# Reordering VectorE's work in an attention stage, and staging its queries in four tiles

## What is computed

```
qh, kh, vh = proj(layernorm(x), Wq, bq), proj(ctx, Wk, bk), proj(ctx, Wv, bv)   # (b, h, s, dk=16, m=4), 16 heads
qh, kh, vh = t + 0.1 * amp * einsum('bhsdi,hij->bhsdj', t, interference)         # for each t of the three
scores = einsum('bhqdm,bhkdm->bhqkm', qh, kh) / sqrt(dk)
out = einsum('bhqkm,bhkdm->bhqdm', softmax(scores, axis=3), vh)
x = x + tanh(g_xattn) * (out @ Wo.T + bo)
y = layernorm(x)
x = x + tanh(g_ffn) * (y @ W_org.T + sum_e coeffs[b, e] * (y @ down[e]) @ up[e])
```

## Time and profile before

| what | before |
|---|---|
| median of 3 runs | 1434.46 us (1432.31 to 1436.73) |
| profiled execution: its own time | 1435.46 us |
| profiled execution: span from first to last instruction | 1433.4 us |
| TensorE busy, share of the span | 1375.1 us, 96% |
| VectorE, ScalarE, GpSimd busy | 672.0, 399.9, 385.8 us |
| mean granted TensorE clock | 0.983 |

### The profile page before, as it was taken

One profiled execution on the slowest core, in us unless ns is written; L12 is line 12 of the kernel. 1 busy time (PEld: TensorE's weight loads), 2 busy tenths in 40 slices (PEclk: granted clock), 3 DMA queues, 4 the chain that ended last, 5 costly groups with the idle time before them and its releaser, 6 DMA issues.

```text
span 1433.4 us, 22180 instructions
## 1 busy us (share of the span) xinstructions
PE 1375.1 (96%) x8464; PEld 1139.6 (80%) x8464; DVE 672.0 (47%) x1370; ACT 399.9 (28%) x728; POOL 385.8 (27%) x584
## 2 busy tenths in 40 slices
PE   7999999999999999779999999999989999999998
PEld 6888888888788888658877888888767878878787
DVE  5333131231855554456666666767766343143110
ACT  3310111111322222234555455555442120121100
POOL 1079990000500000124555565555500000000000
PEclk9999999999999999769999999999999999999999
DMA  5784655636567878976777777775542212202001
GB/s 196 206 223 159 137 150 141 159 133 142 145 190 178 189 165 220 267 209 185 234 211 212 226 208 227 214 214 175 192 153 82 89 45 88 74 31 82 35 31 58
DMA packets 181864, 224.99 MB, mean 157 GB/s; under 512 B 24064, under 2 KB 122496, under 8 KB 181760
## 3 DMA queue, kind: packets, MB, share of 16 engines
q1 hardware_dynamic: 165376, 187.62, 46.1%
q10 hardware_dynamic: 16384, 35.97, 8.0%
HBM read 137.02 MB, written 85.46 MB: 155 GB/s over the span
## 4 chain that ended last, share of the span: by engine, by line
PE 83%; DMA 6%; DVE 5%; issue 2%; SPq 1%; ACT 1%; POOL 0%; ACTq 0%; POOLq 0%; DVEq 0%
PE bank L160 19%; PE bank L162 19%; PE bank L161 19%; PE bank L991 5%; PE bank L976 4%; PE bank L956 4%; DMA early_q<-neg 3%; PE bank L937 3%; PE bank L939 3%; PE bank L938 3%; PE bank L300 2%; PE bank L334 2%; DMA q_in<-neg 2%; DMA q_rows<-stage_hi 1%; DVE raw_o L1139 1%
## 5 line engine op out<-in xcount | busy, mean ns | idle before, releaser
L1057 ACT ACTIVATE probT<-bank 128x512 f32<-128x512 f32 x256 | 139.0, 596 | 100.9 <-PE bank L976 97.2
L1099 DVE TRANSPOSE_TENSOR_REDUCE part<-bank 128x16 f32<-128x512 f32 x256 | 164.3, 672 | 1.9 <-PE bank L956 1.9
L520 DVE SCALAR_TENSOR_TENSOR stage_lo<-bank,bias_mixed,stage_hi 128x512 fp32r<-128x512 f32 x64 | 47.9, 749 | 229.4 <-ACT stage_hi L522 229.4
L160 PE MATMUL bank<-place_a,w_hi 128*128 128x512 f32 x384 | 151.0, 393 | 1.8 <-DVE place_a L153 1.8
L162 PE MATMUL bank<-place_a,w_lo 128*128 128x512 f32 x384 | 149.6, 390 | 0.0
L161 PE MATMUL bank<-place_a,w_hi 128*128 128x512 f32 x384 | 149.5, 389 | 0.0
L522 ACT ACTIVATE stage_hi<-bank,bias_mixed 128x512 fp32r<-128x512 f32 x64 | 44.1, 690 | 273.7 <-PE bank L162 256.1
L937 PE MATMUL bank<-place_a,oT_hi 128*128 128x512 f32 x256 | 108.6, 424 | 0.5 <-POOL oT_lo L1187 0.4
L1443 DVE SCALAR_TENSOR_TENSOR raw_d<-bank,gates,raw_d 128x512 f32<-128x512 f32 x32 | 24.0, 750 | 173.4 <-PE bank L162 173.4
L160 PE MATMUL bank<-place_a,yT_hi 128*128 128x512 f32 x256 | 102.4, 400 | 0.0
L1112 DVE TENSOR_REDUCE negmax<-bank 32x32 f32<-32x128 f32 x128 | 35.6, 278 | 140.0 <-PE bank L963 140.0
(11 more groups left out here) (209 smaller groups left out, 2826.1 us busy)
## 6 DMA issues: line engine op xcount, KB each, us to landing
k_rows<-stage_hi SPq DMA_DIRECT2D x128, 128.0 KB, 2.5
v_pad<-v_out SPq DMA_DIRECT2D x32, 512.0 KB, 2.6
v_place<-v_pad ACTq DMA_DIRECT2D x32, 512.0 KB, 4.9
q_rows<-stage_hi SPq DMA_DIRECT2D x124, 128.0 KB, 2.5
q_in<-q_rows SPq DMA_DIRECT2D x128, 100.0 KB
k_in<-k_rows SPq DMA_DIRECT2D x64, 196.0 KB
early_q<-q_rows SPq DMA_DIRECT2D x90, 100.0 KB
k_rows<-stage_lo SPq DMA_DIRECT2D x64, 128.0 KB, 2.5
```

Source lines behind the costliest of these rows:

```text
L160: nc.tensor.matmul(bank_ap, sh, mh, start=(i == 0), stop=False)
L520: lambda bank: nc.vector.scalar_tensor_tensor(out=lo[:], in0=bank[:], scalar=bias, in1=hi[:].bitcast(F32), op0=ALU.add, op1=ALU.subtract),
L1057: act.activation(probT[o % NPT][:, i].rearrange("k a p q -> k (a p q)"), two_bank[i][:], ACT.Exp).then_inc(s_exp, 1)
L1099: dve.tensor_reduce(part[o % NS][:, :, 2 * i:2 * i + 2, :].rearrange("k a p b -> k a (p b)"), one_bank[i][:].rearrange("k (a b t) -> k a b ...
```

## The change

VectorE's list in a slot becomes: partial maxima; `raw_o` (lag 3), `inv` (lag 4), `raw_s` (lag 1), `sums_t` (lag 2); minimum; reciprocals (lag 3). The queries are staged in four tiles, two of which lie in `wq_own`, with semaphores of their own. ScalarE issues the stores of the last two query chunks, then an exponential of one element, and waits for all stores in slot 3 behind the exponentials of oct 0. SyncE waits in slot 3 only for the stores of the first query group, and for all in slot 11. `part`, `negmax` and `neg` have six tiles each.

```diff
-        idle = sb("idle", [1, 1])
+        idle, warm = sb("idle", [1, 1]), sb("warm", [1, 1])
...
+            key_stage = list(zip(stage_hi, stage_lo))
+            query_stage = key_stage + [(t[:, 0:GT].bitcast(F32R), t[:, GT:2 * GT].bitcast(F32R)) for t in wq_own[1:]]
             s_stage = [sem(f"s_stage{i}") for i in range(2)]
+            s_qstage = [sem(f"s_qstage{i}") for i in range(4)]
...
                 def stage_free(act):
                     if use:
-                        act.wait_ge(s_stage[slot], 96 * use)
+                        act.wait_ge(sems[slot], 96 * use)
+                    elif queries and slot < 2:
+                        act.wait_ge(s_stage[slot], 48 * NG * KC)
+                    elif queries:
+                        act.wait_ge(line.emptied, wq_end[slot - 1])
...
-                if (scratch is q_rows) and (g, c) == (NG - 1, KC - 1):
-                    last_store.append(store)
+                if queries and g == NG - 1 and c >= KC - 2:
+                    last_stores.append(store)
...
+            def first_rows(eng, o):
+
+                eng.wait_ge(s_stage[o % 2], 48 * NG * KC)
+                eng.wait_ge(s_qstage[o % 4], 96 * (o // 4 + 1))
...
-            NS = 3
+            NS = 6
...
                     if s + AHEAD == KQ:
+                        for o in range(KC):
+                            first_rows(sp, o)
+                    if s + AHEAD == GB * NOCT // 2:
                         projected(sp)
...
-                for store in last_store:
+                for store in last_stores:
                     store(act)
-                projected(act)
+                act.activation(warm[:], gates[0:1, 0:1], ACT.Exp)
                 for s in range(SLOTS):
...
+                    if s == LAG:
+                        projected(act)
                     if s in (3, 5, 8, 11):
                         load_v((3, 5, 8, 11).index(s))
...
                         partial_max(s, 1)
-                        dve.wait_ge(s_fold, s + 1)
-                        if s >= NS:
-                            dve.wait_ge(s_nlo, s - NS + 1)
-                        dve.tensor_reduce(negmax[at][:], one_bank[1][0:32, 0:P].rearrange("c (i q) -> c q i", i=4), AX.X,
-                                          ALU.min).then_inc(s_max, 1)
...
+                    h = half_at(s, 3)
+                    if h is not None:
+                        dve.wait_ge(s_o0, h + 1)
+                        dve.scalar_tensor_tensor(out=raw_o[:], in0=v_bank[1][:], scalar=side[:, 1:2], in1=raw_o[:],
+                                                 op0=ALU.mult, op1=ALU.add).then_inc(s_o, 1)
...
                         dve.transpose(sums_t[:], raw_s[:]).then_inc(s_turn, 1)
+                    if s < OCTS:
+                        dve.wait_ge(s_fold, s + 1)
+                        if s >= NS:
+                            dve.wait_ge(s_nlo, s - NS + 1)
+                        dve.tensor_reduce(negmax[at][:], one_bank[1][0:32, 0:P].rearrange("c (i q) -> c q i", i=4), AX.X,
+                                          ALU.min).then_inc(s_max, 1)
...
                             dve.reciprocal(rec[:, :, a:a + 1], by_head[:, :, 1 - a, 0:1]).then_inc(s_rec, 1)
-                        dve.wait_ge(s_o0, h + 1)
-                        dve.scalar_tensor_tensor(out=raw_o[:], in0=v_bank[1][:], scalar=side[:, 1:2], in1=raw_o[:],
-                                                 op0=ALU.mult, op1=ALU.add).then_inc(s_o, 1)
```

More of the change, by code:

```diff
@@ L495, in x_jobs @@
                 t_end[NB + b] = transpose_jobs(line, tin[b % 2], norm.done(b), hi[:, b % GB, :, :], lo[:, b % GB, :, :])
-            staged, last_store = [0], []
+            staged, last_stores = {"keys": 0, "queries": 0}, []
             def projection_job(weight_end, input_end, second_half, hi_in, lo_in, bias, scratch, c, g, lo_section):
-                slot, use = staged[0] % 2, staged[0] // 2
-                staged[0] += 1
-                hi, lo = stage_hi[slot], stage_lo[slot]
+                queries = scratch is q_rows
+                tiles, sems = (query_stage, s_qstage) if queries else (key_stage, s_stage)
+                count = staged["queries" if queries else "keys"]
+                staged["queries" if queries else "keys"] += 1
+                slot, use = count % len(tiles), count // len(tiles)
+                hi, lo = tiles[slot]
                 def moving(k):
@@ L534, in store @@
                                 src[a * 64:(a + 1) * 64, :].rearrange("f (b t) -> f b t", t=P).bitcast(F32)
-                            ).then_inc(s_stage[slot], 16)
-                if (scratch is q_rows) and (g, c) == (NG - 1, KC - 1):
-                    last_store.append(store)
+                            ).then_inc(sems[slot], 16)
+                if queries and g == NG - 1 and c >= KC - 2:
+                    last_stores.append(store)
                 else:
@@ L782, in load_early @@
                             act.wait_ge(s_cleared, EARLY)
-                            act.wait_ge(s_stage[o % 2], 96 * ((NG * KC + o) // 2 + 1))
+                            first_rows(act, o)
                             load_kq(act, o, (first_k, second_k, early_k[2], early_k[3])[o],
@@ L796, in projected @@
                 for i in range(2):
-                    eng.wait_ge(s_stage[i], 96 * NG * KC)
+                    eng.wait_ge(s_stage[i], 48 * NG * KC)
                     eng.wait_ge(s_vst[i], 16 * NB)
+                for i in range(4):
+                    eng.wait_ge(s_qstage[i], 24 * NG * KC)
         wo_hi, wo_lo = place_a, place_c
@@ L877, in load_oct @@
                         sp.wait_ge(s_zero[o % 2], (o - EARLY) // 2 + 1)
-                        sp.wait_ge(s_stage[o % 2], 96 * ((NG * KC + o) // 2 + 1))
+                        first_rows(sp, o)
                     else:
@@ L1108, in _ @@
                         partial_max(s, 1)
-                        dve.wait_ge(s_fold, s + 1)
-                        if s >= NS:
-                            dve.wait_ge(s_nlo, s - NS + 1)
-                        dve.tensor_reduce(negmax[at][:], one_bank[1][0:32, 0:P].rearrange("c (i q) -> c q i", i=4), AX.X,
-                                          ALU.min).then_inc(s_max, 1)
-                    if s == FIRST_V:
-                        dve.wait_ge(s_bo, 16)
-                        dve.tensor_scalar(bo_row[:], bo_row[:], gates[:, 0:1], None, ALU.mult).then_inc(s_bog, 1)
+                    h = half_at(s, 3)
[3 more added lines that the diff above has]
+                                                 op0=ALU.mult, op1=ALU.add).then_inc(s_o, 1)
                     h = half_at(s, 4)
@@ L1131, in _ @@
                         dve.transpose(sums_t[:], raw_s[:]).then_inc(s_turn, 1)
+                    if s < OCTS:
[4 more added lines that the diff above has]
+                                          ALU.min).then_inc(s_max, 1)
+                    if s == FIRST_V:
+                        dve.wait_ge(s_bo, 16)
+                        dve.tensor_scalar(bo_row[:], bo_row[:], gates[:, 0:1], None, ALU.mult).then_inc(s_bog, 1)
                     h = half_at(s, 3)
```

## The result

The changed kernel takes 1419.6 us (median of 4 runs, 1417.46 to 1420.49) where the kernel before, run beside it, takes 1435.6. The ratio is 0.9885, with a 95% interval of 0.9855 to 0.9914: some 16.0 us less, and the predicted 1419.6 us. The forecast was 14.9 us less than 1434.46; the kernel before has a median 1.1 us higher here, so part of the exact agreement is chance. The steps that led to that figure did less well than the figure.

A forecast was written before the change was run, and what follows sets the result against it. TensorE was taken to bound the attention, so gains come from its gaps. Value steps 12.2, tight merge 1 and opening 3.2, less 1.5 for busier queues, gave 14.9 us: 1419.6 us as a median, range 1411 to 1430.

The forecast's parts named there:

- The value steps: Attention: values stop waiting for VectorE's merge into `raw_o`, 0.45 us at each of 27 steps, 12.2 us gained.
- The tight merge: The merge into `raw_s`, moved before the minimum with 0.38 us of idle: 1 us gained, bounds +3 and -9.9.
- Rival D: The merge into `raw_s` delays the minimum by 0.3 us in its slot, 31 times: 1430.5 us; chance 0.11.
- Six tiles of maxima: Attention: removes GpSimd's wait on the DMA of three octs before, which has mostly landed: 0 us.
- The transfers: Attention: stalls behind the maxima's DMA stay where they are; busier queues cost 1.5 us, bounds 0 and 9.4.
- rival C: Shorter attention periods make the maxima's DMA late in most: 2.36 us each, 1444 us with 11 more stalls; chance 0.05.
- The opening: From projections to first values: earlier staging and ScalarE's later store wait bring first values at 611.2, 3.2 us gained.
- rival A: The opening gives nothing, as the wait for all stores, fed by twelve, ends where it did: 1422.8 us; chance 0.10.

The follow-up runs named there:

- e3: The kernel before with only the merge into `raw_o` moved ahead of the minimum: 1427.72 us, ratio 0.9945.
- e2: The changed kernel with VectorE's old order, all else of the change kept: 1430.16 us, ratio 0.9958.
- e5: The changed kernel with three tiles of maxima instead of six: 1417.05 us, ratio 0.9886.
- e6: The kernel before with VectorE's new order and six tiles of maxima, opening and staging as before: 1427.16 us, ratio 0.9954.
- e11: The changed kernel with its warming exponential written into `idle`, so all tiles behind stand 32 bytes lower, as before: 1427.44 us, ratio 0.9938.
- e1: The kernel before with VectorE's whole new order alone: 1428.42 us, ratio 0.9952.
- e9: The kernel before with one unused tile of four bytes, which shifts the tiles behind it by 32 bytes: 1430.09 us, ratio 0.9956.
- e10: The kernel before with VectorE's new order and the unused tile of four bytes, opening and staging as before: 1418.75 us, ratio 0.9885.
- e8: The changed kernel with SyncE again storing the chunk before the last, so ScalarE issues six stores, not twelve: 1417.9 us, ratio 0.9879.
- e12: The changed kernel with first value load ahead of stores, value slots' maxima DMA before the next oct's loads, `down_rows` load two slots later: 1410.71 us, ratio 0.9827.

## Why the prediction was right, and where it wasn't

- **The value steps** (12.2 us, 0.45 us each): right in mechanism and size. The wait is gone, the undisturbed period fell by 0.50 us (12.57 to 12.07), and the distance from pair to values is 0.33 us, between the two ends that were given (0.24 and 0.40). e3, with 0.43 us a period, shows that it is this one instruction. e2 keeps the old order and keeps 28 waits with 10.3 us.
- **The tight merge** (1 us, bounds +3 and -9.9): right. The minimum still waits for the fold, the three others together give 0.07 us a period, 2 us, and TensorE waits for the minimum as often as before, 13 times with 5.1 us (list above) against 13 times with 4.8 us before. Rival D is refuted.
- **Six tiles of maxima** (0): right (e5, e6).
- **The transfers** (1.5 us lost): this step failed, and was mis-sized by far. It said that the stalls stay where they are because the stretch that covers the maxima's DMA isn't shortened. The stretch did keep its length but for 0.1 us (6.10 against 6.18). Yet with the tiles where they were, the stalls grew: by 4.5 and 5.8 us in e6 and e11, by 10.6 in the long execution of e1. At the new place they grew by 3.4 us (e9 to e10). By the medians the order gives 7 us there, of the 12.2 + 1 - 1.5 = 11.7 that were forecast for it, and half of what its periods promise (31 x 0.5 = 15.5 us). That is rival C's mechanism in 11 of some 31 periods, where C had asked for most, at a place of the tiles which the changed kernel no longer has. C had a chance of 0.05. Why the stalls grew although the stretch kept its length, no run shows.
- **The opening** (3.2 us): failed. Its early steps came true and ended in new waits: the last store landed at 605.7 and not 604.5, the load of values issued behind it took 7.99 and not 4.9 us, and behind those two stands the maxima's DMA of oct 3 (0.71 us of waiting in the changed kernel, 1.64 in e8). The median of 4.9 us was taken over the whole run, while the opening has its DMA engines 0.87 busy. By e2 against e9 (0.9958 and 0.9956) and the changed kernel against e10 (0.9885 each), staging and opening together give nothing that shows; e11 against e1 (0.9938 and 0.9952) would allow 2 us, within the intervals. The traces allow as much: from the end of the projections to the first values it takes 22.0 to 25.3 us in the changed kernel, e2, e5 and e11, and 23.7 to 27.0 us in the seven kernels with the old opening, 1.4 us less in the mean. e2 comes to 22.0, near the 21.6 that the forecast amounts to, so the step can come true in one execution. Taken as a whole this is rival A.
- **The four bytes** (not in the sum): worth 6 to 10 us. Of the change's 16 us the order at the old place gives 7 and the shift the rest; counted the other way round, the shift gives 6 and the order at the new place 10.

So the total was right by luck: a gain of some 9 us that wasn't seen stood in for two shortfalls, 3 us of the opening and 5 of the order (7 instead of 11.7).

## What to carry to other kernels

When an instruction of one engine frees a bank for another, put it ahead of a wait that it doesn't need; the timeline shows the room, and the gain per period could be read from it here (0.45 us forecast, 0.43 measured in e3). But a gain per period isn't yet a gain in time where a small transfer has little slack: measure the stalls before and after, and try to issue the small, urgent transfer ahead of the large ones (part of e12, not tried apart). And an added tile, however small, moves all tiles behind it: compare with a kernel that has only that shift before crediting the edit that came with it.

## What the runs showed of the hardware

- Moving the tiles by 32 bytes in SBUF, those of the attention from 32 off a multiple of 64 to a multiple of 64, with no other difference, made the kernel before 0.44% faster (e9) and the kernel with the new order 0.67% (e10 against e1, 0.9885 and 0.9952); moving them back made the changed kernel 0.5% slower (e11, 0.9938). How it works is open.
- The load of the exponential's table took 1.28 us, and an exponential followed it after 1.29 us (599.69 to 600.98; in the kernel before 603.50 to 604.79), without the further 1.38 us of drain that the Trainium skill (ScalarE: Activation LUTs, What ACT_TABLE_LOAD costs) gives; the measurement decides.
- Twelve stores in a row kept ScalarE's queue for 9.54 us, 0.80 us each; a load of 512 KB, issued behind them, took 7.99 us to land where the median of its kind is 4.9 us.
